# Unpacking 4-bit weights inside the feed-forward's first block instead of in a stage of its own

## What is computed

```python
def _dequant(qweight, scales, qzeros, g_idx):
    w = (qw[:, None, :] >> shifts[None, :, None] & MAXQ).reshape(-1, qweight.shape[1])
    z = ((qz[:, :, None] >> shifts[None, None, :] & MAXQ) + 1).reshape(qzeros.shape[0], -1)
    s = scales[g_idx]
    return (w - z[g_idx]) * s
Wg, Wu, Wd = ...            # 512x1376, 512x1376, 1376x512
h = silu(xf @ Wg) * (xf @ Wu)
out = h @ Wd
```

## Time and profile before

| | before |
|---|---|
| time, median of 3 | 1435.1 us (1435.0 to 1439.16) |
| the profiled execution | 1437.98 us, span 1436.2 us |
| PE busy | 1287.4 us (90%) |
| DVE busy | 744.5 us (52%) |
| ACT busy | 569.7 us (40%) |
| POOL busy | 297.9 us (21%) |
| mean granted clock of TensorE | 0.932 |

### The profile page before, as it was taken

How to read it: one execution, slowest core, us unless ns; L and a number is a source line. 1 busy time by engine, 2 the same in 40 slices (tenths; PEclk the granted TensorE clock), 3 DMA queues, 4 the chain that set the end, 5 groups by cost and what they waited for, 6 DMA issues and landing times. The chain is left out here.

```text
span 1436.2 us, 17020 instructions
## 1 busy us (share of the span) xinstructions
PE 1287.4 (90%) x6139; PEld 844.0 (59%) x6178; DVE 744.5 (52%) x1354; ACT 569.7 (40%) x993; POOL 297.9 (21%) x309
## 2 busy tenths in 40 slices
PE   4599999999999999998965859999999999669996
PEld 4566456556545655544432327878878788436664
DVE  4285885885787888632116972132141141365554
ACT  5144454465366555555732431111111111134443
POOL 0122121120110100110231541111121121105554
PEclk9899999899999999999985559999999999879998
DMA  6524222202301211022005321002020020040303
GB/s 189 114 48 113 39 67 75 39 2 60 56 21 25 39 24 34 23 38 26 30 30 131 104 93 59 1 17 72 1 89 1 0 88 0 30 130 1 105 13 117
DMA packets 55677, 76.99 MB, mean 54 GB/s; under 512 B 13072, under 2 KB 30744, under 8 KB 55528
## 3 DMA queue, kind: packets, MB, share of 16 engines
q1 hardware_dynamic: 51984, 65.39, 18.8%
q0 software_dynamic: 2560, 8.39, 1.8%
q10 hardware_dynamic: 1056, 2.16, 0.4%
HBM read 54.44 MB, written 21.59 MB: 53 GB/s over the span
## 5 line engine op out<-in xcount | busy, mean ns | idle before, releaser
L792 DVE TENSOR_REDUCE mx<-bank 128x1 f32<-128x512 f32 (+2 forms) x576 | 367.6, 686 | 141.4 <-PE bank L910 77.1
L734 ACT ACTIVATE PT<-ST 128x512 f32<-128x512 f32 x576 | 313.5, 601 | 213.0 <-PE ST L975 93.7
L907 PE MATMUL bank<-KS,QS 126*128 126x512 f32 (+2 forms) x896 | 254.3, 367 | 19.0 <-DMA QS<-pos_scratch 16.6
L975 PE MATMUL ST<-QS,KS 128*128 128x512 f32 x576 | 241.1, 459 | 4.9 <-DMA QS<-mparts 3.9
L907 PEld LDWEIGHTS bank<-KS,QS 126*128 126x128 f32 x896 | 159.8, 198 | 83.8 <-DVE mx L792 37.8
L1442 DVE TENSOR_TENSOR f_h<-f_h,f_pair 128x512 f32<-128x512 f32 (+1 forms) x44 | 30.3, 689 | 246.3 <-ACT f_h L1387 246.3
L975 PEld LDWEIGHTS ST<-QS,KS 128*128 128x128 f32 x576 | 108.9, 196 | 82.6 <-ACT PT L734 63.3
L989 PE MATMUL PO<-PT,V 128*32 128x512 f32 x1152 | 152.3, 604 | 1.6 <-ACT PT L734 1.6
L51 PE MATMUL f_pair<-f_xT,gu 128*128 128x512 f32 (+1 forms) x352 | 139.5, 396 | 2.1 <-DVE f_xT L1420 1.5
L52 PE MATMUL f_pair<-f_xT,gu 128*128 128x512 f32 (+1 forms) x352 | 139.5, 396 | 0.0
L53 PE MATMUL f_pair<-f_xT,gu 128*128 128x512 f32 (+1 forms) x352 | 139.0, 395 | 0.0
(11 more groups left out here) (179 smaller groups left out, 1811.7 us busy)
## 6 DMA issues: line engine op xcount, KB each, us to landing
QS<-q_scratch SPq DMA_DIRECT2D x48, 256.0 KB
q_scratch<-QP SPq DMA_DIRECT2D x24, 256.0 KB, 2.3
l_x<-x_dram SPq DMA_DIRECT2D x12, 512.0 KB, 4.2
f_xin<-x_dram SPq DMA_DIRECT2D x5, 1024.0 KB, 7.3
xres<-_attn_hidden_states_dram POOLq DMA_DIRECT2D x16, 256.0 KB, 3.2
x_dram<-xout POOLq DMA_DIRECT2D x16, 256.0 KB, 2.4
f_xsum<-x_dram SPq DMA_DIRECT2D x4, 1024.0 KB, 6.0
x_dram<-f_xsum SPq DMA_DIRECT2D x4, 1024.0 KB, 5.2
```

The lines of the kernel that those rows point to most:

```text
L734: act.activation(PT[:, quad % PT_RING, n % 4, :], ST[:, n % ST_RING, :], ACT.Exp).then_inc(p_done, 1)
L792: v.tensor_reduce(mx[:, i % 2, z, h:h + m], at(u).rearrange("p (m k) -> p m k", m=m), AX.X, ALU.max).then_inc(bank_free_dve, 1)
L907: last = pe.matmul(at(u)[:, j * w:(j + 1) * w], hi(QS[0:ROWS1, slot, h + j, :]), hi(KS[b][0:ROWS1, k0:k0 + w]), start=(j == 0 or not diag) ...
L975: last = pe.matmul(dst, hi(KS[b][0:ROWS2, kb * P:(kb + 1) * P]), hi(QS[0:ROWS2, slot, h:h + 4, :]), start=True, stop=not diag)
```

## The change

`dequantize` is gone, and so is the barrier behind it. `ffn` does the unpacking, by pairs of column tiles: pair p holds the gate and up columns and the down rows of tiles 2p and 2p+1. Six pairs of three units (gate, up, down) make 18 units, each 1024 columns of codes (the last pair: 384, 384 and 512), and 33 pieces of at most 512 columns. Pair 0, 6 pieces, is made before the first block. The other 27 are made during the first block of rows, up to three in a column tile, each pair two tiles ahead of its use:

```diff
+def pieces_during(n):
+    p = n // 2 + 1
+    mine = [j for j, (u, _) in enumerate(DQ) if UNITS[u][0] == p]
+    return mine[0:3] if n % 2 == 0 else mine[3:6]
...
+def ffn_events(blk):
+    events = []
+    for n in range(NT):
+        dq = [("dq", j) for j in pieces_during(n)] if blk == 0 else []
+        events += dq[0:1] + [("gate", n)] + dq[1:2] + [("up", n)] + dq[2:3]
+        turns = []
+        if blk == 0 and n >= NT - 2:
+            turns = [("xt", 2 * (n - NT + 2)), ("xt", 2 * (n - NT + 2) + 1)]
+        elif 0 < blk < FB - 1 and n in (3, 5, 7, 9):
+            turns = [("xt", (n - 3) // 2)]
+        events += turns[0:1] + ([("down", n - 1)] if n else []) + turns[1:2]
+    return events + [("down", NT - 1)]
```

A piece of gate or up holds 256 columns of two row chunks, so its zero points and scales take two matmuls each; a piece of down takes one each. The last pair's gate and up take four of 96 columns each:

```diff
+            def weight_piece(j):
+                taken(pe, ("dq", 0, j))
+                pe.wait_ge(q4_done, u + 1)
+                pe.matmul(value[:, 0:n], identb[0:r, 0:r], q4[0:r, u % CODE_RING, a:a + n], start=True, stop=False, skip_group_check=True)
...
+                for k, c in enumerate(cs):
+                    pick = onehotT[:, DQ_COL[m] + c, 0:r]
+                    pe.matmul(value[:, k * w:(k + 1) * w], pick, ztab[:, cols], start=False, stop=True, skip_group_check=True)
+                    last = pe.matmul(scale[:, k * w:(k + 1) * w], pick, stab[:, cols], start=True, stop=True, skip_group_check=True)
+                last.then_inc(picked, 1)
```

The tables are bfloat16 and span all 128 partitions, zero where there is nothing; the scales are now three bfloat16 parts, so `stab` fills 54 partitions. In ACT's and DVE's programs each piece is now done whole:

```diff
+            def weight_copy(j):
+                act.wait_ge(picked, j + 1)
+                if j >= WF_RING:
+                    act.wait_ge(w_lo, j - WF_RING + 1)
+                act.activation(product(j), in_bank(j, 0), ACT.Copy).then_inc(wf_done, 1)
+            def weight_high(j):
+                act.wait_ge(mul_done, j + 1)
+                act.activation(hi(weights(0, j)), product(j), ACT.Copy).then_inc(w_hi, 1)
...
+                    if kind == "dq":
+                        weight_copy(n)
+                        weight_high(n)
...
+                    if kind == "dq":
+                        weight_scale(n)
+                        if codes_after(n) is not None:
+                            codes(codes_after(n))
```

`codes_after` gives, behind the last piece of unit u, the unit u+2: its shift and mask and its cast follow there on DVE. Before the first block the three splitting steps of the scales run ACT, DVE, ACT, DVE, and the zero points are unpacked in two halves in between:

```diff
+            act.wait_ge(s_in, 16 * 9)
+            act.activation(s_part, s_raw, ACT.Copy).then_inc(s_part_done, 1)
+            act.wait_ge(s_rest, 1)
+            act.activation(s_part, s_raw, ACT.Copy).then_inc(s_part_done, 1)
...
+            v.wait_ge(s_part_done, 1)
+            v.scalar_tensor_tensor(s_raw, s_part, group_ids[0:S_ROWS, S_ROWS:S_ROWS + 1], s_raw, ALU.mult, ALU.add).then_inc(s_rest, 1)
...
+            v.wait_ge(s_part_done, 2)
+            v.scalar_tensor_tensor(stab[0:S_ROWS], s_part, group_ids[0:S_ROWS, S_ROWS + 1:S_ROWS + 2], s_raw, ALU.mult, ALU.add).then_inc(tables_done, 1)
...
+            for u in range(CODE_RING):
+                codes(u)
+            row_moments(0)
+            normalize(0)
+            for j in EARLY_PIECES:
+                weight_scale(j)
+                if codes_after(j) is not None:
+                    codes(codes_after(j))
+            for t in range(4):
+                xt_lo(0, t)
```

More of the change, by code:

```diff
@@ L1029, in group_index_loads, with use_before @@
+SLOT_OF = dict(zip(PAIR_USES, PAIR_SLOTS))
+def use_before(use):
+    k = PAIR_USES.index(use)
+    before = [x for x, s in zip(PAIR_USES[:k], PAIR_SLOTS[:k]) if s == PAIR_SLOTS[k]]
+    return before[-1] if before else None
 def group_index_loads(mats, gidx):
@@ L1061, in dequantize @@
[L1061 to L1073, removed]
@@ L1087, in dequantize @@
[L1087 to L1101, removed]
@@ L1103, in size @@
[L1103 to L1132, removed]
@@ L1308, in ffn, with banks, taken @@
         block = ctx.enter_context(nc.Block())
-        def number(blk, e):
-            return blk * F_PER + (4 + F_USES[e])
-        def pair_of(r, e):
-            return pair[:, (4 + r * F_PER + F_USES[e]) % 2, :, :]
-        def rows(dram, row):
-            return dram[bass.ds(row, HALF), :].rearrange("(t p) d -> p t d", p=P)
+        def banks(use):
+            return pair[:, SLOT_OF[use], :, :]
+        def taken(eng, use):
+            before = use_before(use)
+            if before is None:
+                return
+            kind, blk, n = before
+            if kind == "dq":
+                eng.wait_ge(mul_done, n + 1)
+            elif kind == "gate":
+                eng.wait_ge(h_ready, blk * NT + n + 1)
+            else:
+                eng.wait_ge(xt_lo_done, 4 * blk + n + 1)
@@ new lines, in down @@
+            def down(blk, n):
+                w, s = tile_w(n), slot(blk, n)
+                pe.wait_ge(h_lo, blk * NT + n + 1)
+                if blk == 0:
+                    pe.wait_ge(w_lo, pieces_before(n // 2, 2))
+                elif n == 0:
+                    pe.wait_ge(y_ready, 4 * blk)
+                for t in range(4):
+                    at = slice(t * P, (t + 1) * P)
+                    pe.matmul(Y[:, t, :], hi(h_parts[0][0:w, s, at]), hi(wd[0][0:w, n, :]), start=(n == 0), stop=False)
+                    pe.matmul(Y[:, t, :], hi(h_parts[0][0:w, s, at]), hi(wd[1][0:w, n, :]), start=False, stop=False)
+                    last = pe.matmul(Y[:, t, :], hi(h_parts[1][0:w, s, at]), hi(wd[0][0:w, n, :]), start=False, stop=(n == NT - 1))
+                    if n == NT - 1 and t < 3:
+                        last.then_inc(y_tile, 1)
+                last.then_inc(down_done, 1)
@@ new lines, in _ @@
+            pe.wait_ge(onehot_done, 1)
+            for a in range(DQ_COLS):
+                if a == 16:
+                    pe.wait_ge(onehotT_done, 1)
+                pe.matmul(turn[:, a // 4 % 4, a % 4 * P:(a % 4 + 1) * P], onehot[:, a, :], identb[:, :], start=True, stop=True).then_inc(onehot_turned, 1)
+            pe.wait_ge(onehotT_done, -(-DQ_COLS // 4))
+            pe.wait_ge(tables_done, 2)
+            for j in EARLY_PIECES:
+                weight_piece(j)
+            for t in range(4):
+                transposes(0, t)
@@ L1522 @@
+            for blk in range(FB):
+                for kind, n in ffn_events(blk):
+                    if kind == "dq":
+                        weight_piece(n)
+                    elif kind == "xt":
+                        transposes(blk + 1, n)
+                    elif kind == "down":
+                        down(blk, n)
+                    else:
+                        project(blk, 0 if kind == "gate" else 1, n)
 BLK = 32
```

616 lines of the change are left out of this document (312 added, 304 removed).

## The result

The changed kernel took **1401.9 us** (median of 4 runs, 1395.9 to 1402.1) against 1435.05 us for the kernel before in the same session (4 runs): a ratio of 0.976, 95% interval 0.974 to 0.978. The forecast was 1409.5 with a range of 1396 to 1431. The profiled execution of after took 1395.92 us against 1437.98 of before.

The account below looks back on a forecast made before the run. The prediction took the feed-forward as bound by PE alone, with everything ahead of its first gate matmul paid in full. Terms: -56.2 + 23.2 + 10.9 - 3.6 = -25.7 us, giving 1409.5 us, range 1396 to 1431.

Parts of the forecast that it names:

- The start: Stretch ahead of block 0's first gate matmul: that matmul at 806.5 us (800 to 816), 56 us earlier.
- tables done: In the stretch before the first gate matmul: scale and zero-point tables complete at 774.1 us, before codes may load.
- The pieces: Block 0: 27 unpacking pieces add PE work of 0.86 us each, 23.2 us in all (18.7 to 31).
- The rival of bare loads: Block 0's pieces: weight loads don't hide, so they cost 31 us instead of 23; 1416 us, chance 0.10.
- The waits: Block 0: PE waits where DVE and ACT finish a tile before its third piece, 10.9 us (5 to 25).
- Tile 0: Block 0's first tile: PE waits 4.1 us, having no down as cover and a Silu table load of 1.28.
- Codes steps: Block 0, even tiles: DVE's shift and cast, delayed by POOL, run about 0.6 us late four times, 2.4 us.
- Saved elsewhere: Two PE waits of 0.7 us and 16 transposes of the unused fifth block go, saving 3.6 us together.
- The port: DVE and POOL obstruct each other in every block 0 tile, 14 us more waiting; 1423 us, chance 0.18.
- Low clock in block 0: TensorE's clock stays at its lower level throughout block 0, +100 us; 1510 us, chance 0.05.
- Late start: First gate matmul at 816 instead of 806.5 us, as early pieces pass four engines in turn; 1419 us, chance 0.10.
- not hidden: Block 0's pieces each cost PE the old stage's 2.0 us, 54 us in all; 1440 us, chance 0.07.

Follow-up runs that it names:

- the repeat: The changed kernel run again unaltered on another chip to see its spread: 1399.6 us, ratio 0.975 to the kernel before.
- rows first: Changed kernel with block 0's row moments and normalisation ahead of the first two codes steps on DVE: 1396.0 us, ratio 0.972 to the kernel before.

## Why the prediction was right, and where its sizes were off

The sign, the mechanism and the order of the terms held: the first gate matmul came earlier by most of the old stage, block 0 paid part of it back, blocks 1 to 3 stood nearly as before. With all pieces ahead of the gate the time was 1423.7, which shows that the hiding makes 1.5 of the 2.4 points. The forecast was 8 us too high, and each of its three large terms erred the same way.

1. **The start** (predicted 49.75 us from the feed-forward's start, measured 46.36). The scales came 1.1 early, the tables 1.0 (16.3 against 17.35), and 0.4 more was gained up to the end of normalisation. From there to the gate I had 17.0; it was 15.1. Early pieces run at 1.8 us each, with the casts at 1.58 as the POOL wait foresaw. The term "tables done" was right in size for a partly wrong reason: I put the scales' arrival on the path, while DVE, held by POOL's clears, was there just as late, with no idle time from 753.45 to 769.7. So the clearing that the prediction priced at nothing beside the loads (and at 4 us uncovered; the three large clears lasted 5.9) seems to have been on the path, through DVE. With the conversion moved the stall moved along, so its price is not measured; a version with the clears elsewhere was not tried.

2. **The pieces** (23.2 predicted, about 17.6 measured: block 0's 25.0 less 7.4 of waits, 0.65 each; 0.67 by the spacing above). This is the term that was most mis-sized. My nearest row, the pattern of 0.86 in attention, was too dear, and the lower bound of 0.69 was no bound either: picks of 256 columns follow each other in 0.11, so a piece is 0.23 and four times 0.11, a little under three starts of 0.23. The rival of bare loads had its price of 31 nearly right: without padding block 0 took 37.3 more than before, and 5.1 of that were waits. It is the padding that kept it away. The prediction took that from rows in which all loads use 128 rows; the rows with bare loads had 18 and 36.

3. **The waits** (10.9 predicted, 7.4 measured). Tile 0: 4.1 predicted, 3.13 measured; the table load, 1.28 in my sum, gave back 0.13 when it was moved away, since DVE's cast ended as late. Tile 1: 1.9 and 1.58. Tile 2: 1.9 and 2.20. Codes steps: 2.4 and 0.5. Tiles 9 and 10: 0.6 and nothing that PE shows as a wait. The engines' loads in a tile were also set too high for ACT, 8.6 us, where it was busy for 48.8 in eleven tiles, 4.4 each; nothing in the sum hung on it. The chain of 3.66 us against PE's 3.64 was the right picture: moving the pieces one place removed tile 0's pause, cutting up the statistics removed those of tiles 1 and 2.

4. **Saved elsewhere** (3.6 predicted). Blocks 1 to 3 and layer 1's first matmul gave 1.0, 0.4 and 2.1, in sum 3.5.

5. **The rivals.** The port: DVE's casts do stand 1.05 us each, 10.5 in all, but cutting POOL's work gave 1 us in the start and 2.6 to 3.2 in block 0, not 14. (The medians of the two kernels stand 7.1 apart; what is beyond these 4 the feed-forward's stages don't show.) Low clock in block 0: 0.98 on the mean; it was low in the first 2 us (0.56 from 799.73 to 801.90) and after one pause. Late start and not hidden: no.

The sum by its own steps: start -3.4, pieces -5.6, waits -3.5 against the forecast, 12.5 of the 13.0 between -25.7 and -38.7. The medians, though, stand 33.2 apart and those of the repeat 35.9, where the profiled pair stands 42.1 apart. Before was profiled in an execution 2.9 above its median, and after in one 6.0 below its own; 3.4 of these 8.9 us are attention's start. So the stages overstate the gain by 3 to 6 us, and in which of them the excess lies is not shown. The three errors are errors of the terms against this pair of profiles.

## What to carry to other kernels

Work of other engines hidden beside a full TensorE costs what TensorE itself must do for it (27 pieces at 0.67) and the places where a hand-over chain has less cover than length; list those places with their slack, since they, not the engines' totals, decide. When a wait is removed, look whether another engine or the clock takes it back: a table load moved away was replaced by a cast that ended as late, and 1.2 us less of waiting by a second clock loss. And before an instruction is moved off a stalled engine, ask what holds it: here the stall simply fell on the next one.

## What the runs showed of the hardware

- A DVE operation on 128x18 numbers took 5.9 us, and one on 128x4 numbers 5.6 us, beside a row of POOL memsets that followed each other (1.23, 3.50 and 1.24 us); both ended with the last large one and did not slip in between; before, beside one memset of 1.23, the first took 1.27. That the memsets are the cause is read from the ends that agree; no run moved the memsets. A shift of 0.75 took 1.53 where a subtraction had begun 0.3 us before it (rows first, 787.80), and 0.75 where the shift was first (785.78); there the subtraction took 1.66 instead of 1.30. Statistics of the same engine (0.68 us each) did not stand for POOL's subtractions, nor did multiplies from PSUM (0.69).
- Weight loads of 128 rows hide under matmuls of 128 rows (picks 0.11 apart), and so do loads of 96 under 96 and of 128 under 96 (0.23 and 0.22); loads in the sequence of 128, 18 and 54 rows do not (0.21 apart, and 0.23 idle before the first). Padding with zero rows made the kernel 13 us faster.
- After a PE pause of 2.0 to 3.1 us the granted clock was 0.67 for 5.1 us in some cases and full in others, a loss of 1.7 us each time, enough to mask the effect of an edit of that size.
